# Mixing a batch in 16 chunks of 16 tokens in place of 8 of 32, on one core

## What is computed

```
h = layernorm(patches(x)) * gamma + beta, times W, plus b             # [16, 255, 256]
h = h + attn(layernorm(h))
h = h + ffn(layernorm(h))                                             # each token: the one best of 8 experts

attn:  b = (q * k).sum(-1) * SCALE;  a = -softplus(alpha).sum(-1)    # a score and a decay per token and head
       ln_t = log(exp(a_t + ln_(t-1)) + exp(b_t))                    # scan over the tokens, 8 heads
       s_t  = exp(a_t) * s_(t-1) + exp(b_t) * v_t                    # the same decay, a vector of 256 for each head
       y_t  = sum over heads of s_t / exp(ln_t);   return y @ W_o.T
```

## Time and profile before

| | |
|---|---|
| Runs | 593.19 us median of 3 (591.73 to 594.14) |
| Profiled execution | 592.6 us, of which 590.8 us is the span shown in the profile |
| TensorE busy | 527.1 us (89% of the span) |
| VectorE busy | 471.5 us (80%) |
| ScalarE busy | 229.7 us (39%) |
| GpSimd busy | 197.6 us (33%) |
| Granted clock of TensorE, mean | 0.979 of full speed |

### The profile page before, as it was taken

One profiled execution on the slowest core, in us unless ns is written; L12 is line 12 of the kernel. 1 busy time (PEld: TensorE's weight loads), 2 busy tenths in 40 slices (PEclk: granted clock), 3 DMA queues, 4 the chain that ended last, 5 costly groups with the idle time before them and its releaser, 6 DMA issues. The chain is left out here.

```text
span 590.8 us, 12977 instructions
## 1 busy us (share of the span) xinstructions
PE 527.1 (89%) x3457; PEld 371.3 (63%) x3458; DVE 471.5 (80%) x1212; ACT 229.7 (39%) x439; POOL 197.6 (33%) x276
## 2 busy tenths in 40 slices
PE   2988999999999999999869799999588988988982
PEld 2865667777666677776526666675355765765661
DVE  2757888898888888988998999997667877877771
ACT  1335445455654544656443211111033433434440
POOL 2463232322223222221230222231225555555532
PEclk9989999999999999999989999999879999999997
DMA  9211212221222122111231233323412222222210
GB/s 252 97 37 37 73 40 67 71 71 36 71 71 68 39 71 71 57 50 36 50 113 44 89 98 108 117 73 126 161 36 71 74 62 76 62 63 68 65 43 1
DMA packets 32682, 43.04 MB, mean 73 GB/s; under 512 B 7234, under 2 KB 23859, under 8 KB 32400
## 3 DMA queue, kind: packets, MB, share of 16 engines
q1 hardware_dynamic: 22604, 28.11, 15.0%
q0 software_dynamic: 3744, 9.34, 5.5%
q10 hardware_dynamic: 6308, 5.28, 3.1%
HBM read 34.02 MB, written 9.59 MB: 74 GB/s over the span
## 5 line engine op out<-in xcount | busy, mean ns | idle before, releaser
L518 PE MATMUL banks<-proj,xnT_h 128*128 128x512 f16 x384 | 115.6, 383 | 6.2 <-DVE early L1220 6.2
L499 PE MATMUL banks<-early 128*128 128x256 f16 x768 | 88.5, 276 | 2.6 <-DVE wo_l L1049 2.6
L499 PEld LDWEIGHTS banks<-early 128*128 128x128 f16 x768 | 76.0, 99 | 12.0 <-DVE wo_l L1049 2.9
L518 PE MATMUL banks<-proj,xnT_l 128*128 128x512 f16 x192 | 73.3, 382 | 0.0
L518 PEld LDWEIGHTS banks<-proj,xnT_h 128*128 128x128 f16 x384 | 37.5, 98 | 43.5 <-DVE early L1220 7.4
L1848 POOL DMA_INDIRECT out<-proj,vo x39 | 39.6, 1016 | 65.2 <-DVE vo L1679 47.9
L747 PE MATMUL banks<-w2h,vo 128*128 x312 | 57.6, 273 | 4.0 <-DVE proj L1677 3.5
L728 PE MATMUL banks<-w1h,vo 128*128 x156 | 54.5, 391 | 7.4 <-issue 4.9
L1842 POOL DMA_INDIRECT vo<-token_rows,vo x39 | 42.4, 1086 | 28.0 <-issue 28.0
L996 ACT ACTIVATE vo<-banks 128x256 f16<-128x256 f32 x39 | 15.0, 384 | 90.9 <-PE banks L715 66.5
L1833 POOL TENSOR_TENSOR rows<-rows,minus_half 128x1 f32 x32 | 23.5, 735 | 74.9 <-DVE rows L1517 74.9
(11 more groups left out here) (258 smaller groups left out, 1276.3 us busy)
## 6 DMA issues: line engine op xcount, KB each, us to landing
early<-in_x SPq DMA_DIRECT2D x16, 512.0 KB, 3.4
stage<-in_W SPq DMA_DIRECT2D x32, 256.0 KB, 2.8
early<-lam_by_chunk SPq DMA_DIRECT2D x32, 132.0 KB
token_rows<-rows ACTq DMA_DIRECT2D x16, 129.0 KB, 2.6
rows<-in_b SPq DMA_DIRECT2D x1, 2048.0 KB, 7.0
token_rows<-rows ACTq DMA_DIRECT2D x16, 112.9 KB, 2.0
vo<-in_tok_W ACTq DMA_DIRECT2D x2, 512.0 KB, 7.1
early<-lam_by_head SPq DMA_DIRECT2D x16, 64.0 KB
```

The costliest lines, as they stand in the source:

```text
L499: last = mm(bank(2 + j, D), x_[:, k, at:at + P], w[:, KG * half + k, :], start=(half == 0 and k == 0 and x_ is gT_h and w is wtok_h), stop ...
L518: last = mm(dst, a, c, start=(i == 0), stop=(i == n - 1))
```

## The change

Chunks are 16 tokens long, so a tile has 8 and a batch 16 of them. 16 chunks x 8 heads fill 128 partitions, so `qst`, `lst` and the heads' decays are now per batch, each in two buffers, with one `head_decays` scan for each batch (slots k = 1 and k = 3), one bank of end states for each batch and one copy of it. The heads' decays of pair p - 1 are loaded among the tiles' decays of pair p. `keep_busy(1)` is gone from TensorE's slot. In the last step of the first stage two chunks are before alpha and the third behind it; ScalarE splits the last expert's weights after the first logarithms. GpSimd makes the marks on all partitions at once with a per-partition condition, six of eight rounds ahead of the router's root.

```diff
@@ -54,7 +54,7 @@
 PAIRS = B // 2
-CH = 32
+CH = 16
 NCH = 2 * P // CH
@@ -194,14 +194,14 @@
         lam_tile = early[:, 0:4 * HEADS * SPAN].rearrange("p (k f) -> p k f", k=4)
-        lam_head = early[:, 4 * HEADS * SPAN:4 * HEADS * SPAN + 2 * P]
+        lam_head = early[:, 4 * HEADS * SPAN:4 * HEADS * SPAN + 4 * P].rearrange("p (w t) -> p w t", w=2)
         resp = sb("resp", [P, HEADS + 1, SPAN])
         wsum = sb("wsum", [P, 2, CH])
         wbd = sb("wbd", [P, 4, P])
         ends = sb("ends", [P, 4, P])
-        qst = sb("qst", [P, 2 * P])
+        qst = sb("qst", [P, 2, 2 * P])
         hT = early[:, 1536:2560].rearrange("p (w f) -> p w f", w=4)
-        lst = sb("lst", [P, MIXC])
+        lst = sb("lst", [P, 2, MIXC])
...
@@ -375,23 +375,24 @@
-            def load_head_decays(p, first=False):
+            def load_head_decays(p, half, first=False):
                 if not first:
-                    sp_.wait_ge(s["q_done"], p)
-                for half in range(2):
-                    sp_.dma_start(lam_head[64 * half:64 * half + 64, :],
-                                  lam_by_head.rearrange("(b h) t -> b h t", h=HEADS)[2 * p + half]
-                                  .unsqueeze(0).to_broadcast([NCH, HEADS, 2 * P])).then_inc(s["lam_head_in"], 16)
+                    sp_.wait_ge(s["q_done"], 2 * p + half - 1)
+                sp_.dma_start(lam_head[:, half, :],
+                              lam_by_head.rearrange("(b h) t -> b h t", h=HEADS)[2 * p + half]
+                              .unsqueeze(0).to_broadcast([NCH, HEADS, 2 * P])).then_inc(s[f"lam_head_in_{half}"], 16)
             for k in range(4):
                 load_tile_decays(0, k, True)
-            load_head_decays(0, True)
+            for half in range(2):
+                load_head_decays(0, half, True)
             load_expert_part(B - 1)
             def load_decays(p):
                 for k in range(4):
                     load_tile_decays(p, k)
-                load_head_decays(p)
+                    if p > 1 and k % 2 == 0:
+                        load_head_decays(p - 1, k // 2)
@@ -402,6 +403,8 @@
                 load_decays(p)
+            for half in range(2):
+                load_head_decays(PAIRS - 1, half)
@@ -641,31 +644,31 @@
                 pe.wait_ge(s["ends_ready"], apart(pe, 4 * p + k + 1))
-                if k == 0 and not (isinstance(p, int) and p == 0):
-                    pe.wait_ge(s["l_copied"], p)
+                n = 2 * p + k // 2
+                if k % 2 == 0 and n > 0:
+                    pe.wait_ge(s["l_copied"], n)
                 if p == PAIRS - 1 and k == 2:
                     pe.wait_ge(s["vo_copied"], TILES)
-                last = mm(bank(4, MIXC), ends[:, k, :], vo[:, 4 * p + k, :], start=(k == 0), stop=(k == 3))
-                if k == 3:
+                last = mm(bank(4, MIXC), ends[:, k, :], vo[:, 4 * p + k, :], start=(k % 2 == 0), stop=(k % 2 == 1))
+                if k % 2 == 1:
                     last.then_inc(s["l_ready"], 1)
             def mix(p, k):
                 t = 4 * p + k
-                b2_, j = k // 2, k % 2
+                n, j = 2 * p + k // 2, k % 2
                 if not (isinstance(p, int) and t < 2):
                     pe.wait_ge(s["h2_done"], t - 1)
                 pe.wait_ge(s["es_ready"], t + 1)
                 mm(bank(2 + k % 2, MIXC), wbd[:, k, :], vo[:, t, :], start=True, stop=False)
                 hidden_logits(t)
-                if k == 0:
-                    pe.wait_ge(s["q_done"], p + 1)
-                    pe.wait_ge(s["l_copied"], p + 1)
-                mm(bank(2 + k % 2, MIXC), qst[64 * b2_:64 * b2_ + 64, j * P:j * P + P], lst[64 * b2_:64 * b2_ + 64, :],
+                if j == 0:
+                    pe.wait_ge(s["q_done"], n + 1)
+                    pe.wait_ge(s["l_copied"], n + 1)
+                mm(bank(2 + k % 2, MIXC), qst[:, n % 2, j * P:j * P + P], lst[:, n % 2, :],
                    start=False, stop=True).then_inc(s["out_ready"], 1)
             def pair(p, ahead=True):
                 for k in range(4):
-                    keep_busy(1)
                     mix(p, k)
@@ -891,12 +894,12 @@
                     exp_gates(0)
-                if ahead == 0:
-                    split_expert(b)
                 copy_q(b, 0, first)
                 if ahead >= 2:
                     keep_xT(b + 2, 0)
                 log_part(b, 0, first)
+                if ahead == 0:
+                    split_expert(b)
                 copy_q(b, 1)
@@ -926,11 +929,11 @@
-            def keep_ends(p):
-                act.wait_ge(s["l_ready"], p + 1)
-                if not (isinstance(p, int) and p == 0):
-                    act.wait_ge(s["out_ready"], 4 * p)
-                af(lst[:], bank(4, MIXC), ACT.Copy).then_inc(s["l_copied"], 1)
+            def keep_ends(n, w):
+                act.wait_ge(s["l_ready"], n + 1)
+                if not (isinstance(n, int) and n < 2):
+                    act.wait_ge(s["out_ready"], 2 * n - 2)
+                af(lst[:, w, :], bank(4, MIXC), ACT.Copy).then_inc(s["l_copied"], 1)
@@ -946,7 +949,7 @@
             def pair(p, early_on=False):
-                keep_ends(p)
+                keep_ends(2 * p + 1, 1)
                 keep_hT(4 * p + 1, 1)
@@ -957,6 +960,7 @@
                     keep_vo_last(1)
+                keep_ends(2 * p + 2, 0)
                 keep_hT(4 * p + 3, 3)
@@ -964,9 +968,11 @@
             keep_hT(1, 1)
-            keep_ends(0)
+            keep_ends(0, 0)
+            keep_ends(1, 1)
             keep_hT(2, 2)
             split_v(B - 1)
+            keep_ends(2, 0)
             keep_hT(3, 3)
@@ -975,7 +981,7 @@
                 pair(p)
-            keep_ends(PAIRS - 1)
+            keep_ends(B - 1, 1)
             for k in range(1, 4):
@@ -1321,9 +1327,9 @@
                     k = self.k
-                    col = 64 * (k // 2) + CH * (k % 2)
+                    col = HEADS * CT * (k % 2)
                     end = resp[:, 0:HEADS, CH:SPAN].rearrange("p h s -> p (h s)")
-                    stt(ends[:, k, col:col + CH].rearrange("p (c h) -> p c h", c=CT), repeated(end, [P, CT, HEADS]),
+                    stt(ends[:, k, col:col + HEADS * CT].rearrange("p (c h) -> p c h", c=CT), repeated(end, [P, CT, HEADS]),
                         last_row[:], mask4[:], ALU.add, ALU.mult).then_inc(s["ends_ready"], 1)
@@ -1332,10 +1338,10 @@
-            def head_decays(p):
-                dve.wait_ge(s["lam_head_in"], 32 * p + 32)
-
-                scan(qst[:], head_state_in[:], lam_head, 0.0, ALU.add, ALU.mult).then_inc(s["q_done"], 1)
+            def head_decays(p, half):
+                dve.wait_ge(s[f"lam_head_in_{half}"], 16 * p + 16)
+
+                scan(qst[:, half], head_state_in[:], lam_head[:, half], 0.0, ALU.add, ALU.mult).then_inc(s["q_done"], 1)
@@ -1376,7 +1382,7 @@
                     dve.wait_ge(s["consts2"], 1)
-                    for t in range(3):
+                    for t in range(2):
                         chunk_full(t)
@@ -1391,6 +1397,7 @@
                 if ahead == 0:
+                    chunk_full(2)
                     fourth = chunk_ahead(3)
@@ -1475,7 +1482,7 @@
             gate_b(B - 1, 1)
-            head_decays(0)
+            head_decays(0, 0)
             fifth = chunk_ahead(4)
@@ -1499,8 +1506,10 @@
                 tt(row[:, 2:ROWT], bank(2 + k % 2, MIXC), row[:, 2:ROWT], ALU.add).then_inc(s["h2_done"], 1)
-                if left >= 4 and k == 3:
-                    head_decays(p + 1)
+                if k == 1:
+                    head_decays(p, 1)
+                elif left >= 4 and k == 3:
+                    head_decays(p + 1, 0)
                 if coming:
@@ -1746,13 +1755,29 @@
-            for ap in (chunk_mask, mask4, last_row, decay_in, resp, zeros, not_before,
+            for ap in (last_row, decay_in, resp, zeros, not_before,
                        head_state_in, wsum, ends):
                 clear(ap[:])
-            clear(valid[:], 1.0)
+            for ap in (valid, chunk_mask, mask4):
+                clear(ap[:], 1.0)
             for e in range(E):
                 clear(rank_w[:, e:e + 1], float(E - e))
             select(not_before[:], [[1, P]], -1, -1, GE, -1.0)
+
+            for ap, cols in ((chunk_mask, CH), (mask4, HEADS)):
+                select(ap[:], [[-CH, CT], [0, cols]], 0, 1, GE, 0.0)
+                select(ap[:], [[CH, CT], [0, cols]], CH - 1, -1, GE, 0.0)
+            def mark_chunk(q):
+                made.settle()
+                for ap, pattern, base, value in ((last_row[:], [[0, 1]], -(CH - 1), 1.0),
+                                                 (decay_in[:, :, 1:SPAN], [[0, HEADS], [-1, CH]], 0, -1.0),
+                                                 (resp[:, HEADS, 1:SPAN], [[-1, CH]], 0, float(HEADS))):
+                    made.step(g.affine_select(out=ap, in_=ap, pattern=pattern, compare_op=NE, fill=value, base=base - CH * q,
```

(25 more changed lines are left out.)

4 lines of the change are left out of this document (2 added, 2 removed).

## The result

The changed kernel took 576.34 us as the median of four executions (574.55 to 578.20), beside 593.26 us for the kernel before on the same chip: a ratio of 0.9718, 95% interval 0.9681 to 0.9755, faster. The forecast was 577.5 us, or 0.9735.

A forecast was written before the change was run, and what follows sets the result against it. VectorE was taken to bound the mixing pair at 10.94 us, TensorE following at about 10.0. Slots 9.9 + first stage's last step 3.4 + set-up 1.9 = 15.2 us off 592.6 gave 577.4, stated as 577.5; range 572 to 585.

The forecast's parts named there:

- What bounds the pair: Mixing loop: VectorE sets the pair at 10.94 us, TensorE's four slots take about 10.0; after the change 9.55.
- The slot's price: VectorE's mixing slot: scan saves 0.27 us, sum over heads 0.26, product for the ends grows slightly; net 0.50 less.
- the denser row's rate (0.30): VectorE's sum over heads: alternative bound of 0.30 us, at 1.04 ns an element, if nearer spacing brings that rate.
- The first eight slots, 2.8 us: Start of mixing: eight slots save 0.50 us each, less two extra scans of the heads' decays at 0.60; 2.8 us.
- TensorE at 1.00 through the stage: Mixing stage: TensorE's granted clock stays full without the unread product; a clock below 1 would show the prediction wrong.
- a new wait for l_copied: Mixing stage: waiting for ScalarE's copy of the end states would show the prediction wrong; about 0.75 us counted at the start.
- The clock as a rival on the other side, 0.07: Mixing stage: without the product TensorE runs at half clock, slot 3.8 us, 45 us lost, 622 us total; chance 0.07.
- The start of the mixing, 3.4 us: First stage's last step up to the first mixing slot: shorter chunks, reordering and fewer waits save 3.4 us, bounds 2.3 to 4.5.
- Set-up, 1.9 us: Set-up: marks moved into GpSimd's idle time bring the layernorm's root earlier, ending TensorE's wait for alpha; 1.9 us, bounds 0 to 2.5.
- Last eight slots, 1.5 us: End of mixing: TensorE's slot decides, so the removed product saves 1.8 us, less 0.3 for the extra scan; 1.5.
- TensorE's floor, 2.29 us: Mixing: TensorE's own slot falls from 2.51 to 2.29 us once the unread product of 0.22 is removed.
- Loads and the store: Decays through memory: twice as many store pieces, 68 bytes for 132, and doubled heads' loads were costed at nothing.

The follow-up runs named there:

- the written-out pair: Changed kernel with VectorE's four middle mixing pairs written out in place of a loop: 571.19 us, ratio 0.9668 to the kernel before.
- the filler: Changed kernel with six unread 512-column products added once on TensorE, in its pause behind the gates' reciprocal: 572.94 us, ratio 0.9706 to the kernel before.

## Why the prediction was right, point by point

- **What bounds the pair.** Right. VectorE set it at 10.94 us and sets it at 9.48; the written-out pair shows that VectorE's time still counts in full down to 8.67.
- **The slot's price.** Right to about 0.02 us for each instruction. Scaling the reduce from the row of its own layout gave 0.40 for 0.384; the denser row's rate (0.30) would have been wrong.
- **The first eight slots, 2.8 us.** Too high: 1.4. The step that failed is "TensorE at 1.00 through the stage". I had taken the full clock at 338 us, where TensorE was busy 0.69 of 2 us, as proof for the whole stage. That stretch is the same pause behind the gates' reciprocal, before slot 6. There the clock held; in the changed kernel it fell, and with the product put back it fell too. One execution that passes through such a pause at full clock doesn't show that the next one will. With the filler ahead of it the eight slots took 1.7 us less. A clock below 1 in the stage was one of the prediction's own signs that it is wrong, and so was a new wait for l_copied: both came. The first cost 1.4 us, the second 0.8, which the prediction had put at 0.75.
- **The clock as a rival on the other side, 0.07.** It did not decide here. Its price was sound (a slot of 3.8 us; 3.78 was measured in the stretch at half clock), and what I did not see is that the same removal alone, in the kernel before, loses the clock for 60 us in one profiled execution, with a median 2.4% slower in the second set of four.
- **The start of the mixing, 3.4 us.** Mis-sized: 2.6. The old order in the changed kernel gave the same 2.5. The stretch at half clock that I had taken away with TensorE's pause for alpha did not go but came earlier, at 296 us. The reordering, which I credited with the waits of 0.47 and 0.62 us, only moved them: 0.72 us for alpha and 1.44 behind the handshake stand in their place.
- **Set-up, 1.9 us.** Right in mechanism and size. What the trace gained beyond that, 1.1 us, was TensorE's clock.
- **Last eight slots, 1.5 us.** 2.1; the product's removal is 0.8 of it by the run with the product put back, and 1.0 by the kernel before without it (14.01 us for 15.00), not 1.8. That TensorE's slot decides in all eight was wrong: in the kernel before VectorE still sets the first steps (392.64 - 390.26 = 2.38 us, without a wait), so its shorter slot counts there too.
- **TensorE's floor, 2.29 us.** Too high: 2.00. I had subtracted the product's step and taken every other one as needed, but some of them held idle time: the last step of the slot, for one, took 0.64 us there (396.87 - 396.23) and 0.53 here (355.34 - 354.81).
- **Loads and the store.** No wait of VectorE for decays appears in the mixing stage. The twice as many pieces are hidden.
- **The last 1.5 us** of the profiled difference lie in the routing and the experts, which the change doesn't touch. From the addition of slot 31 to the end of the execution the 14 profiled executions took 182.8 to 187.3 us, the changed kernel's first 185.8 and the kernel before 187.3, so the difference is within what this stretch varies by. What makes it vary stays open.

What stays open: why the clock came back after 6 us in the changed kernel and not for 60 us in the kernel before without its product, though TensorE was busy 2.00 of 2 us in both; and which part of the change lets the changed kernel keep its clock without the product.

## What to carry to other kernels

The same unread filler was needed in one kernel and not in the other. When a change drops one, try its removal alone as well, and look at the clock of several executions, not of one. A long instruction on the engine that sets the pace (here a reciprocal of 1.7 us) is where the engine behind it goes idle and pays afterwards. Count what a loop costs by writing one out: its price is in the steps between instructions as well as in the gap that the view marks.

## What the runs showed of the hardware

- With TensorE at half clock and busy 60.00 of 60 us between 340 and 400 us, the clock stayed at 0.50 (the kernel before without its product, second run).
- Behind a pause of TensorE of some 2 us the clock fell to 0.50 in seven of seven profiled executions of the changed kernel and its variants, and held at 1.00 in four of four in which unread products had shortened the pause (to 0.77 to 0.80 us). In the kernel before it held behind a pause of 1.75 us; without its product, behind 1.97 us, it held in one execution and fell in another.
- VectorE's loop of four pairs cost 0.81 us a pass against the same work written out (9.48 and 8.67 us), of which the view marks 0.35 as idle.
- A VectorE product with two inputs of 0.31 or 0.28 us took 1.07 or 1.26 us when it began beside a two-input GpSimd instruction of 1.15 us.
- The same 24 matmuls of the set-up took 2.79 us in three of 14 profiled executions and 4.04 to 4.46 us in the others: up to 1.7 us of chance, 0.3% of the kernel, before the first stage begins.
